# Row products for q and for the score weights taken in plain float32 from the raw Wq and Wk

## The reference, cut to what matters

```python
q = cond_1024[:, None, :] @ Wq.T + bq          # one row of 512 per batch element, 2 of them
k = x @ Wk.T + bk                              # x is 2 x 2048 x 512
v = x @ Wv.T + bv
# 16 heads of 32 columns; q is divided by sqrt(32)
attn = clip(einsum('bhqd,bhkd->bhqk', q, k), 0.0, 1.0)     # one query: one score for each key and head
out  = x + (attn[..., None] * v as rows of 512) @ Wo.T + bo
```

## Time and profile before

| | |
|---|---|
| median of 3 runs | 185.34 us (184.75 to 185.38) |
| time of the profiled execution | 185.33 us |
| its span in the profile | 183.5 us |
| mean granted TensorE clock | 1.00 of full speed |
| TensorE busy | 179.6 us, 98% of the span |
| VectorE busy | 170.1 us, 93% |
| ScalarE busy | 115.7 us, 63% |
| bytes moved by DMA | 30.15 MB, mean 164 GB/s |

### The profile page before, as it was taken

The page is one execution under the profiler, slowest core; times in us unless marked ns, Lnnn a source line. Parts: engine busy times, 40 slices in busy tenths (PEclk is TensorE's granted clock), DMA queues, the critical chain, the costliest instruction groups (busy, mean ns, idle before and its releaser), DMA issues.

```text
span 183.5 us, 2369 instructions
## 1 busy us (share of the span) xinstructions
PE 179.6 (98%) x795; PEld 146.4 (80%) x795; DVE 170.1 (93%) x188; ACT 115.7 (63%) x158; POOL 14.3 (8%) x20
## 2 busy tenths in 40 slices
PE   8999999999999999999999999999999999999993
PEld 2788788888878888888888888888888888888883
DVE  0899999898899999999999999999999999989963
ACT  3689875587696755675577774693486854766300
POOL 8000000000000020111000010111000001111000
PEclk9999999999999999999999999999999999999999
DMA  6999920115901106499278616489930206579686
GB/s 218 344 387 429 402 79 2 27 32 162 351 17 44 41 17 114 138 161 222 54 278 274 226 28 114 129 155 300 261 131 0 57 0 111 144 135 297 117 352 221
DMA packets 9355, 30.15 MB, mean 164 GB/s; under 512 B 1152, under 2 KB 1536, under 8 KB 9216
## 3 DMA queue, kind: packets, MB, share of 16 engines
q1 hardware_dynamic: 7616, 23.72, 35.7%
q0 software_dynamic: 1728, 6.29, 20.6%
HBM read 19.52 MB, written 8.39 MB: 152 GB/s over the span
## 4 chain that ended last, share of the span: by engine, by line
PE 96%; DMA 2%; ACT 0%; DVE 0%; issue 0%
PE bank_y L354 9%; PE bank_y L356 9%; PE bank_y L358 9%; PE bank_x L354 8%; PE bank_x L358 8%; PE bank_x L356 8%; PE bank_z L354 6%; PE bank_z L358 6%; PE bank_z L356 6%; PE bank_x L429 5%; PE score_bank L415 4%; PE score_bank L414 4%; PE bank_z L429 3%; PE bank_x L449 2%; DMA work<-first_t 2%; PE bank_y L449 1%
## 5 line engine op out<-in xcount | busy, mean ns | idle before, releaser
L582 ACT CAST form_hi<-work 128x1024 fp32r<-128x1024 f32 x28 | 29.1, 1051 | 20.3 <-PE score_bank L415 6.8
L861 DVE TENSOR_TENSOR form_lo<-work,form_hi 128x1024 fp32r<-128x1024 f32 (+1 forms) x38 | 40.3, 1080 | 1.8 <-ACT form_hi L582 1.6
L617 ACT ACTIVATE work<-bank_y,const 128x512 f32<-128x512 f32 x30 | 19.7, 687 | 9.0 <-PE bank_y L358 9.0
L844 POOL DMA_DIRECT2D work<-x_t x12 | 10.5, 874 | 154.0 <-DVE work L894 146.2
L354 PE MATMUL bank_x<-form_hi,wo_hi 128*128 128x512 f32 x52 | 20.3, 391 | 0.0
L358 PE MATMUL bank_x<-form_hi,wo_lo 128*128 128x512 f32 x52 | 20.2, 389 | 0.0
L356 PE MATMUL bank_x<-form_lo,wo_hi 128*128 128x512 f32 x52 | 20.2, 389 | 0.0
L617 ACT ACTIVATE work<-bank_x,const 128x512 f32<-128x512 f32 x24 | 15.9, 684 | 6.3 <-PE bank_x L358 5.7
L883 DVE SCALAR_TENSOR_TENSOR work<-relu,work 128x1024 f32<-128x1024 f32 x16 | 19.4, 1219 | 0.0
L861 DVE TENSOR_TENSOR form_lo<-x_raw,form_hi 128x1024 fp32r<-128x1024 f32 x15 | 18.3, 1219 | 0.8 <-ACT form_hi L582 0.8
L354 PE MATMUL bank_y<-form_hi,wv_hi 128*128 128x512 f32 x48 | 18.7, 389 | 0.0
(11 more groups left out here) (152 smaller groups left out, 387.2 us busy)
## 6 DMA issues: line engine op xcount, KB each, us to landing
x_raw<-x_t SPq DMA_DIRECT2D x16, 512.0 KB, 6.2
out_t<-work SPq DMA_DIRECT2D x14, 512.0 KB, 3.9
work<-x_t POOLq DMA_DIRECT2D x12, 512.0 KB, 5.4
score_others<-score_rows SPq DMA_DIRECT2D x16, 128.0 KB, 2.3
work<-first_t SPq DMA_DIRECT2D x2, 512.0 KB, 3.9
work<-wq_t SPq DMA_DIRECT2D x2, 512.0 KB, 8.3
work<-wk_t SPq DMA_DIRECT2D x2, 512.0 KB, 11.1
work<-wo_t SPq DMA_DIRECT2D x1, 1024.0 KB, 13.5
```

The source lines that it names most:

```text
L582: nc.scalar.copy(flat(form_hi, kind), raw(kind, phase)).then_inc(hi_ready[kind], 1)
L617: nc.scalar.activation(result_set(phase)[:, q, j * ROWS:(j + 1) * ROWS], of[:, j, :], ACT.Identity, bias=bias[:, tile:tile + 1], scale=sca ...
L844: pool.dma_start(output_set(s)[:, q, :], x_t[s, q], accum_op=ALU.add).then_inc(residual_added[q], 16)
L861: return nc.vector.tensor_tensor(to, of, hi.bitcast(F32), ALU.subtract)
```

## The change

- q rows and a rows are taken as plain float32 matmuls, straight from the raw Wq and Wk and from unsplit vectors: four matmuls for q and four for a, where there were eight and eight. The vectors fill 32 array columns (`GROUP`), and the output goes to 32 partitions. cond is padded to 32 columns by the host.
- So the casts and the subtractions of Wq and Wk (`wq_part`, `wk_part`, four and four on ScalarE, the same on VectorE) fall away, as do `split_cond`, the split of q, two memsets and the additions of the hi and lo results in `scale_q` and `fill_a`.
- All transposes now take 32 rows. The transposes for a and the matmul for c move into the product of W21 and T3, before its third term. The a rows go ahead of that product.
- The constants grow from 232 to 320 columns.
- `next_x` is split: the loads of Q11 and Q12 of the next x go ahead of the load of Wo, those of Q22 and Q21 behind it.
- The written-out orders of ScalarE and VectorE are changed in many places. In the first phase ScalarE's Wo casts go later, and `copy_scores(0, 0)` goes behind `first_values(Q22)`, `hi(B11, 1)` and `hi(B21, 1)`. On VectorE `fill_a` and `split_a(0)` go behind `x_t1`, `lo(T1, 1)`, `x_t2`, `x_t3` and one Wo part. Later phases see neighbours exchanged.

```diff
+GROUP = BATCH * HEADS
-        q_psum = score_bank[1][:, 0:2 * MT * BATCH].rearrange("p (m s b) -> p m s b", m=MT, s=2)
-        a_psum = score_bank[1][:, P:3 * P].rearrange("p (k s n) -> p k s n", k=KT, s=2)
-        c_psum = score_bank[1][:, 3 * P:3 * P + MT * BATCH].rearrange("p (m b) -> p m b", m=MT)
+        q_psum = a_psum = score_bank[1][:, 0:MT * GROUP].rearrange("p (m n) -> p m n", m=MT)
+        c_psum = score_bank[0][:, 0:MT * BATCH].rearrange("p (m b) -> p m b", m=MT)
...
+            next_x_upper(1)
             sp.dma_start(wo_raw.rearrange("p t n -> p (t n)"), wo_t.rearrange("p b n -> p (b n)")).then_inc(wo_loaded, 16)
-            next_x(1)
+            next_x_lower(1)
...
-            def rows(out, vectors, hi_semaphore, lo_semaphore):
-                pe.wait_ge(hi_semaphore, KT)
+            def rows(out, vectors, tile):
                 for k in range(KT):
-                    pe.matmul(out[:, :], vectors[:, k, :], qk_tile(form_hi, k), start=k == 0, stop=False)
-                pe.wait_ge(lo_semaphore, KT)
-                for k in range(KT):
-                    mm = pe.matmul(out[:, :], vectors[:, k, :], qk_tile(form_lo, k), start=False, stop=k == KT - 1)
+                    mm = pe.matmul(out[0:GROUP, :], vectors[:, k, :], tile(k), start=k == 0, stop=k == KT - 1)
                 return mm
...
-            pe.wait_ge(cond_ready, 1)
-            rows(q_rows_psum, cond_parts, wq_hi_ready, wq_lo_ready).then_inc(q_rows_done, 1)
+            pe.wait_ge(small_loaded, 16)
+            for loaded in wq_loaded:
+                pe.wait_ge(loaded, 16)
+            rows(q_rows_psum, cond, wq_raw).then_inc(q_rows_done, 1)
...
-            def score_weight_rows():
-                pe.wait_ge(q_parts_ready, 1)
-                rows(a_rows_psum, q_parts, wk_hi_ready, wk_lo_ready).then_inc(a_rows_done, 1)
+            pe.wait_ge(q_ready, 1)
+            for loaded in wk_loaded:
+                pe.wait_ge(loaded, 16)
+            rows(a_rows_psum, q_heads, wk_raw).then_inc(a_rows_done, 1)
+
+            def turn_score_weights():
+                pe.wait_ge(q_ready, 2)
+                pe.wait_ge(a_rows_ready, 1)
+                pe.matmul(c_psum, const[:, C_SAME:C_SAME + P], bk_q[:, :, :], start=True, stop=True)
+                for k in range(KT):
+                    mm = pe.transpose(a_psum[:, k, :], a_rows[0:GROUP, k * P:(k + 1) * P], one)
+                mm.then_inc(a_done, 1)
...
             wv_sum_part(S1, 0)
-            wq_part(0)
-            wq_part(1)
             wv_sum_part(S2, 1)
-            wq_part(2)
-            wq_part(3)
+            wv_sum_part(S4, 2)
             first_hi(T3, Q12)
...
-            wk_part(0)
             copy_q_rows()
-            wk_part(1)
-            wk_part(2)
-            wk_part(3)
+            hi(T1, 1)
+            first_values(Q12, banks[2], 4)
+            copy_a_rows()
             wo_part(W11, 0)
             wo_part(W12, 1)
+            wo_part(W22, 3)
+            hi(T2, 1)
+            wv_sum_part(S3, 3)
+            first_values(Q22, banks[0], 6)
+            hi(B11, 1)
+            hi(B21, 1)
+            copy_scores(0, 0)
```

More of the change, by code:

```diff
@@ L410, in scores @@
                     parts = ((T3, 0), (B22, 4))
+                if half and s:
+                    operand_ready(B22, VALUES_AT[s])
                 for kind, at in parts:
@@ L423, in first_product @@
                     terms = [terms[0], terms[2], terms[1]]
-                for w, y in terms:
+                for n, (w, y) in enumerate(terms):
+                    if between and n == 2:
+                        between()
                     pe.wait_ge((wv_lo_ready if w is wv_lo else wv_hi_ready)[form], 2 if form in first_w else 1)
@@ L490, in _ @@
             for m in range(MT):
-                n = 2 * BATCH
-                mm = pe.transpose(q_psum[:, m, :, :], q_rows[0:n, m * P:(m + 1) * P], const[0:n, C_ONE:C_ONE + n])
+                mm = pe.transpose(q_psum[:, m, :], q_rows[0:GROUP, m * P:(m + 1) * P], one)
             mm.then_inc(q_done, 1)
             first_product(banks[2], W12, B22, False, True)
-            def score_weight_rows():
-                pe.wait_ge(q_parts_ready, 1)
-                rows(a_rows_psum, q_parts, wk_hi_ready, wk_lo_ready).then_inc(a_rows_done, 1)
-            pe.wait_ge(first_out[Q11], 2)
[L502 to L510, removed]
+            pe.wait_ge(q_ready, 1)
[9 more added lines that the diff above has]
+                mm.then_inc(a_done, 1)
+            pe.wait_ge(first_out[Q11], 2)
+            first_product(banks[0], W21, T3, True, False, between=turn_score_weights).then_inc(w21_done, 1)
             first_product(banks[0], W22, B22, False, True)
             pe.wait_ge(a_ready, 3)
+            pe.wait_ge(c_ready, 1)
             scores(0, 0).then_inc(score_done, 1)
             product_t1(1)
-            pe.wait_ge(c_ready, 1)
             scores(0, 1).then_inc(score_done, 1)
@@ L573, in hi @@
                 before, s_before = PHASES[phase - 1]
-                if phase == 1 and kind in (T1, T2):
-                    act.wait_ge(a_rows_done, 1)
-                elif before == VALUES and kind in FIRST_PHASE_KINDS and (kind != B22 or s_before == 0):
+                if before == VALUES and kind in FIRST_PHASE_KINDS and (kind != B22 or s_before == 0):
                     act.wait_ge(score_done, score_number(s_before, kind in (T3, B22)) + 1)
@@ L730, in _ @@
             first_values(Q21, banks[1], 2)
-            wk_part(0)
             copy_q_rows()
-            wk_part(1)
-            wk_part(2)
-            wk_part(3)
+            hi(T1, 1)
+            first_values(Q12, banks[2], 4)
+            copy_a_rows()
             wo_part(W11, 0)
             wo_part(W12, 1)
-            wo_sum_part(S1, 0)
[L739 to L751, removed]
+            wo_part(W22, 3)
[5 more added lines that the diff above has]
+            copy_scores(0, 0)
+            hi(T4, 1)
+            wo_sum_part(S2, 1)
+            wo_sum_part(S1, 0)
             hi(T3, 1)
             copy_scores(0, 1)
+            hi(B22, 1)
             copy_b11(1)
-            hi(B22, 1)
+            wo_sum_part(S3, 2)
+            wo_sum_part(S4, 3)
             relu_scores(0, 0)
@@ L1159, in _ @@
             wv_sum_part(S4, 2)
-            wk_part(0)
-            wk_part(1)
-            wk_part(2)
-            wk_part(3)
-            wo_sum(0)
+            first_lo(T3, Q12)
+            first_lo(B22, Q22)
             scale_q()
+            scale_bk()
             x_t1(1)
-            scale_bk()
-            wo_sum(1)
+            lo(T1, 1)
+            x_t2(1)
             x_t3(1)
             wo_part(W11, 0)
+            fill_a()
+            sum_c()
+            split_a(0)
             wo_part(W12, 1)
-            wo_sum_part(S2, 1)
-            wo_sum(2)
-            fill_a()
-            split_a(0)
-            lo(T1, 1)
-            x_t2(1)
+            lo(T2, 1)
             wv_sum_part(S3, 3)
-            sum_c()
-            wo_sum(3)
-            lo(T2, 1)
+            x_t4(1)
+            wo_sum(0)
+            wo_sum(1)
             lo(B11, 1)
-            x_t4(1)
             lo(B21, 1)
             lo(T4, 1)
+            wo_sum(2)
             lo(T3, 1)
+            wo_sum_part(S2, 1)
+            lo(B22, 1)
+            wo_sum(3)
             sum_scores(0, 0)
-            lo(B22, 1)
+            wo_sum_part(S1, 0)
+            context(0, Q11)
             add_out11(1)
-            context(0, Q11)
+            context(0, Q21)
             sum_scores(0, 1)
-            context(0, Q21)
+            wo_sum_part(S3, 2)
             lo(B11, 2)
@@ L1202, in _ @@
             lo(T2, 2)
-            wo_sum_part(S1, 0)
             lo(T3, 2)
             add_out12(1)
-            wo_sum_part(S3, 2)
             wo_part(W22, 3)
+            lo(B11, 3)
             add_out11(2)
-            lo(B11, 3)
             context_t4(2)
@@ L1234, in _ @@
             context(1, Q21)
+            context(1, Q22)
             add_out22(3)
-            context(1, Q22)
             lo(T1, 4)
@@ L1241, in _ @@
             lo(T2, 4)
+            lo(B11, 5)
             lo(T3, 4)
             add_out12(3)
-            lo(B11, 5)
             context_t4(4)
@@ L1282, in _ @@
             lo(B11, 7)
+            add_out11(6)
+            lo(B22, 6)
             sum_scores(3, 1)
-            add_out11(6)
+            context(3, Q21)
             context(3, Q12)
-            lo(B22, 6)
             context_t1(7)
             context(3, Q22)
+            lo(B21, 7)
             lo(T1, 7)
@@ L1291, in _ @@
             context_t2(7)
-            context(3, Q21)
             context_t3(7)
             lo(T2, 7)
-            lo(B21, 7)
             context_t4(7)
```

145 lines of the change are left out of this document (47 added, 98 removed).

## The result

| | before | changed |
|---|---|---|
| median of 6 runs | 185.25 us | 189.87 us |
| lowest to highest | 184.75 to 185.38 | 188.81 to 190.96 |
| profiled execution, its span | 185.33, 183.5 us | 190.31, 188.5 us |
| TensorE busy | 179.6 us, 98% | 184.1 us, 98% |
| VectorE busy | 170.1 us, 93% | 164.3 us, 87% |

The ratio is 1.0249, 95% interval 1.0228 to 1.0270. The prediction had 188.8 us with a range of 187.0 to 190.6: the time lies inside, the sign and the main mechanism were right, and 4.6 us were lost where 3.5 were forecast. Two more things are to be noted. The changed kernel's six runs are spread over 2.1 us, those of the kernel before over 0.6. And the profiled execution is 0.4 us above the median, with a span 5.0 us longer than before.

A forecast was written before the change was run, and what follows sets the result against it. TensorE's gapless instruction list was taken to bound the kernel. Row products +3.42, switches +0.2 and VectorE's relief -0.1 made +3.5 us, from 185.33 to 188.8 us, 1.9% slower; range 187.0 to 190.6 us.

The forecast's parts named there:

- the main mechanism: Eight float32 row products stream four times each on TensorE, 7.04 us, replacing sixteen float32r matmuls of 3.62 us: +3.42 us.
- the sum itself: The whole change: +3.42 + 0.2 - 0.1 = +3.5 us, giving 188.8 us; bounds 188.4 and 189.8.
- a new wait of TensorE: Rival, 9%: the later `copy_scores(0, 0)` delays the chain to `lo(B11, 2)`; TensorE waits 1 to 3 us, 190 to 192.
- What bounds the kernel: TensorE, busy 98%, runs without gaps from 5 to 180.4 us; work taken from ScalarE or VectorE is worth nothing by itself.
- The price of a float32 product: Row products of q and a: four streams of 512 columns and two instruction costs, 0.88 us each, 7.04 for eight.
- Switches: Entering and leaving the two sets of 32-column float32 row products: +0.2 us, bounds 0 to 0.84.
- Transposes, waits, loads: Transposes of 32 rows net 0; new waits before the scores are covered; reordered loads cost 0.
- The 0.1 us at phase 2: A late matmul at phase 2's start, waiting for its operand's low part: VectorE's relief gains 0.1 us.
- The loads: Wq and Wk land before their use; moving Wo's load behind two x loads costs 0.
- do the new waits hold: Walk of the lists around q and a rows: copies are covered, and nearly 2 us remain before the scores need `a_ready`.
- Two and three streams: Rivals on a float32 row product's price: two streams, 9%, 185.4 us; three, without low by low, 4%, 187.2 us.
- The faster rival: Rival, 6%: a 32-column product's four parts run at once in four array quarters, one stream per tile, 183.6 us.

The follow-up runs named there:

- the wide array: Changed kernel with row products taken from a 128-column array load of constants into all 128 output partitions: 189.49 us, one run.

## Why the prediction was right, and where it was short

- **The number.** 189.87 us lies inside the range, but just above 189.8, the upper end of what the sum itself allowed. It is covered because the range left room for a new wait of TensorE, and that wait didn't come. In this the range was lucky.
- **What bounds the kernel.** Right. TensorE's stream sets the span but for its tail, and 5.8 us less of VectorE's work bought nothing by themselves.
- **The price of a float32 product.** Right in kind, a little high: I took four streams and two instruction costs, 0.88 us; measured 0.86, the low end of the price with four streams. Net of what was removed, 8 x 0.86 - 3.62 = +3.26 us instead of +3.42.
- **Switches.** Too small. I took +0.2 of a bound of 0.84; the wide array showed 0.32 for each excursion, +0.64. The four transposes had shown 0.09 and 0.12 at their edges; the exit of these sets costs 0.23. Why it is more was not tried.
- **Transposes, waits, loads.** Right. The turns cost what they did (0.36 for 0.34 and 0.39), no new wait appeared before the scores, and Wo's place made no difference. 3.26 + 0.64 = 3.90 stands beside the 3.86 that the timeline shows from q rows to scores.
- **The 0.1 us at phase 2.** Wrong. The matmul there starts 55.63 - 55.34 = 0.29 us after its predecessor, where it was 0.28. The low part that this product waits for can't be made sooner by an emptier VectorE: before and after, VectorE sat idle for ScalarE's high part, and ScalarE for TensorE's scores, which still read the old one. From that cast to the matmul it is 51.41 - 48.89 = 2.52 us before and 55.63 - 53.10 = 2.53 after. The first line is of the kernel before, beside the earlier trace rows; the others are of the changed one:

```profile
48.89 1.05 ACT L582 CAST form_hi<-work 128x1024 fp32r<-128x1024 f32 x1 [1.18 <-PE score_bank L415]
```

```profile
53.10 1.06 ACT L574 CAST form_hi<-work 128x1024 fp32r<-128x1024 f32 x1 [1.18 <-PE score_bank L412]
```

```profile
54.19 1.22 DVE L830 TENSOR_TENSOR form_lo<-work,form_hi 128x1024 fp32r<-128x1024 f32 x1 [0.26 <-ACT form_hi L574]
```

```profile
55.34 0.39 PE L353 MATMUL bank_y<-form_hi,wv_lo 128*128 128x512 f32 x1
55.63 0.47 PE L349 MATMUL bank_x<-form_hi,wo_hi 128*128 128x512 f32 x1
```

- **The step that was missing.** "The loads" and "do the new waits hold" end at phase 2. I costed the exchanged neighbours of the later phases at nothing and gave no cover for it. One of them, the addition of Q22's output moved behind two low parts in the last phase, cost 0.9 to 1.1 us (ratios 1.0249 and 1.0259 against 1.0201). It didn't make TensorE wait; it lay behind TensorE's last matmul, in a queue of DMAs, where the covering argument "TensorE never waits" says nothing.
- **The rivals.** Two and three streams are ruled out by 0.86 us a product. A new wait on TensorE didn't come: the delay of `copy_scores(0, 0)` was covered. The faster rival fell for the kernel as changed, and for the reason given, all parts add up in one group; its mechanism is real, and works between products when each has its own group: 1.00 us for four.

The sum with measured terms: 3.86 + 0.9 = 4.8 us against 4.6 between the medians.

## What to carry to other kernels

In a kernel whose TensorE stream has no gap, price a change of data type in streams of the moving matrix, and distrust relief on any other engine. A float32 product of 512 columns cost four streams here, 0.86 us against 0.226 for a float32r matmul. It needed only 32 output rows; with each tile of the contraction in its own group of columns, and the turn adding them up, four cost about the time of one. And when an order list is rewritten, walk it to the last store: the queues of DMAs behind the last matmul have their own bound, which no wait of TensorE shows.

## What the runs showed of the hardware that was not expected

- Four transposes of 128 x 128 float32 elements took 0.36 us between starts (19.77 to 20.13), as long as four of 32 x 32 (0.36) and hardly longer than four of 4 x 4 (0.34); the other four of that size in the same execution took 0.39.
- Entering and leaving a group of 32 columns cost 0.32 us around one set of products, on a stream that has otherwise 0.01 us between matmuls.
- An addition by DMA of 512 KB lands in 5.2 to 6.9 us in most cases, but the last of super 2 took 7.3 to 8.8 us in the five profiles where it followed the first of three by 6.9, and the last of super 1 took 8.2 to 9.6 in all twelve. What it shares the DMA engines with at these times was not parted.
- Four float32 products in four groups of 32 columns took 1.00 us to the next matmul, in one group 3.55.
